# Moving split-off low parts to other engines, one softmax normalisation per step, and a new order of steps in a fused state-space and local-attention kernel

## The reference, cut to what matters

```python
xn = _layernorm(x)                      # x: 16 sequences x 256 tokens x 128
s = state_space_branch(xn)              # projections, convolutions, selective scan
for i in range(6):                      # DEPTH; 16 heads of 64, window of 32 tokens
    x = attn_layer(shift_tokens(x), Wqkv[i], q_scale[i], k_scale[i], Wo[i]) + x
    x = ffn_layer(shift_tokens(x), ln_g[i], ln_b[i], W1[i], b1[i], W2[i], b2[i]) + x
out = x0 + s * silu(x)

def attn_layer(x, Wqkv, qs, ksc, Wo):
    q, k, v = split(x @ Wqkv)           # 3 x 16 heads x 64
    q, k = l2norm(q) * qs, l2norm(k) * ksc
    q = q * cos * scale + rotate_half(q) * sin * scale
    k = k * cos / scale + rotate_half(k) * sin / scale
    return local_attention(q, k, v) @ Wo            # softmax(8 q k) v over a band

def ffn_layer(x, g, bln, W1, b1, W2, b2):
    xn = (x - mean) / sqrt(var + 1e-05) * g + bln
    a, gate = split(xn @ W1 + b1)
    return a * gelu(gate, approximate=False) @ W2 + b2
```

## Time and profile before

| | |
|---|---|
| median of 3 runs | 4315.71 us (4312.8 to 4320.33) |
| the profiled execution's own time | 4310.28 us |
| its span, first to last instruction | 4308.2 us |
| busy: TensorE, VectorE, ScalarE, GpSimd | 85%, 84%, 71%, 63% of the span |
| first and last `nb` instruction (line 1246) | 495.2 and 4219.4 us |

### The profile page before, as it was taken

One profiled execution on the slowest core, in us unless ns is written; L12 is line 12 of the kernel. 1 busy time (PEld: TensorE's weight loads), 2 busy tenths in 40 slices (PEclk: granted clock), 3 DMA queues, 4 the chain that ended last, 5 costly groups with the idle time before them and its releaser, 6 DMA issues. The chain is left out here.

```text
span 4308.2 us, 109724 instructions
## 1 busy us (share of the span) xinstructions
PE 3648.7 (85%) x31072; PEld 2319.1 (54%) x31072; DVE 3618.5 (84%) x12131; ACT 3063.5 (71%) x8807; POOL 2732.3 (63%) x4419
## 2 busy tenths in 40 slices
PE   5887688898888888888988888888888888898884
PEld 2444355555555555555555555555555555555552
DVE  7999688889888888888888888888887888888873
ACT  3443477777777777777787777777776777877774
POOL 0000577777777777677776776777776767777771
PEclk8999799999999999999999999999999999999997
DMA  1000322222222222222222222222222222222221
GB/s 45 6 7 12 106 92 90 85 90 96 90 88 90 82 95 93 87 93 84 84 101 91 93 87 80 88 95 88 99 84 79 94 95 89 94 85 89 86 78 61
DMA packets 225228, 352.55 MB, mean 82 GB/s; under 512 B 41535, under 2 KB 68349, under 8 KB 224381
## 3 DMA queue, kind: packets, MB, share of 16 engines
q1 hardware_dynamic: 224604, 345.22, 23.4%
HBM read 125.41 MB, written 5.77 MB: 30 GB/s over the span
## 5 line engine op out<-in xcount | busy, mean ns | idle before, releaser
L964 POOL TENSOR_SCALAR pr<-pr,rden 128x128 f32<-128x128 f32 (+1 forms) x3072 | 1134.4, 388 | 931.7 <-DVE rden L1219 930.6
L852 ACT ACTIVATE pr<-sm,nb,rq 128x128 f32<-128x128 f32 (+1 forms) x3072 | 1515.9, 498 | 44.7 <-DVE nb L1246 39.4
L971 POOL TENSOR_TENSOR rot<-ab,swp 128x512 f32<-128x512 f32 x768 | 984.4, 1282 | 509.7 <-DMA swp<-ab 508.5
L1194 DVE TENSOR_TENSOR ab<-bank,ltab 128x512 f32<-128x512 f32 x1536 | 985.4, 683 | 281.3 <-PE bank L292 260.8
L1240 DVE CUSTOM_DVE_ANT_0 sm<-bank,mask 128x128 f32<-128x128 f32 (+1 forms) x3072 | 841.3, 330 | 55.9 <-issue 52.2
L840 ACT ACTIVATE sq<-bank 128x512 f32<-128x512 f32 x768 | 451.6, 588 | 256.7 <-DVE ab L1194 255.0
L852 ACT ACTIVATION_READ_ACCUMULATOR pr<-sm,nb,rq 128x1 f32 x3072 | 587.8, 191 | 0.0
L634 PE MATMUL bank<-ident,pr 128*128 128x128 f32 x1536 | 407.1, 291 | 210.1 <-DVE pt L1226 208.3
L1226 DVE COPY pt<-bank 128x512 f32<-128x512 f32 x768 | 531.5, 692 | 10.2
L625 PEld LDWEIGHTS bank<-rot 64*64 64x64 f32 x12288 | 291.9, 133 | 452.8 <-issue 452.4
L977 POOL TENSOR_TENSOR rot<-rot,rkb 128x512 f32<-128x512 f32 x384 | 497.7, 1296 | 44.2 <-DMA rkb<-k_scratch 44.2
(11 more groups left out here) (156 smaller groups left out, 6503.7 us busy)
## 6 DMA issues: line engine op xcount, KB each, us to landing
swp<-ab SPq DMA_DIRECT2D x1536, 128.0 KB, 2.0
rkb<-k_scratch SPq DMA_DIRECT2D x768, 128.0 KB, 2.9
raw<-Wqkv SPq DMA_DIRECT2D x48, 128.0 KB, 2.2
gg<-xT SPq DMA_DIRECT2D x48, 128.0 KB, 2.3
gg<-xT SPq DMA_DIRECT2D x48, 127.5 KB, 2.4
raw<-Wqkv SPq DMA_DIRECT2D x12, 256.0 KB, 2.7
wo<-Wo SPq DMA_DIRECT2D x6, 512.0 KB, 4.2
k_scratch<-rsum SPq DMA_DIRECT2D x192, 8.0 KB
```

The source lines that it names most:

```text
L852: ins = act.activation(pr[:, s % 4, i, cs], sm[:, s % 2, i, cs], ACT.Exp, bias=nb[:, s, t, i:i + 1], scale=head_scale(rq, p, b)[:, t, i:i ...
L964: ins = pool.tensor_scalar(pr[:, e % 4, i, cs], pr[:, e % 4, i, cs], rden[:, e, t, i:i + 1], 1.0, ALU.mult, ALU.mult)
L971: pool.tensor_tensor(rot[:, PAIRS * (j % 2) + j // 2, :], ab[:, j % 2, 0, :], swp[:, j % 2, :], ALU.add).then_inc(qk_rot, 1)
L1194: ins = dve.tensor_tensor(seqs(ab[:, j % 2, i, :]), seqs(use_bank("qk", j)[:, :]), ltab[:, 2 * (j % 2) + i:2 * (j % 2) + i + 1, :] .to_bro ...
```

## The change

- x's parts for the group after next are no longer made on VectorE. `shift_next` (SyncE, step 8) writes the shifted x to a new buffer `xs2` with two DMAs, ScalarE makes the high part in one copy of 128x512 (step 11), GpSimd the low part in one subtraction (step 13).
- `split_low` of the weights moves from VectorE to GpSimd.
- `gate` is gone: Gelu reads the gate's bank itself, with the bias, so the gates' banks are free only after Gelu.
- `normalise` is one `tensor_tensor` per step, over 2x2x160 columns with `rden` broadcast, in place of four `tensor_scalar` of 128 or 160 columns. `pr` has 160 columns for each tile, the unused 32 being zero.
- Bank 7 is also used by q/k block 4 and gate 2; the sums of quads 0 and 2 become a use of that bank.
- Order: `cen` goes from TensorE's step 7 to 8, sum group 2 from 13 to 14, group 3 from 1 to 0, the third `dn` from 2 to 3, `norms(0)` from 9 to 8 on ScalarE; on VectorE `clamp` and `gated` come ahead of `maxima`, and `scale_q` one step earlier; GpSimd's `scale_k` of pair 7 goes from step 12 to 13, those of pairs 5 and 6 go one step earlier; k's norms go to DRAM one step earlier. `xs` has its own buffer, so that its zero column is written once.

```diff
-              [("prev", "cen", 0, 6), ("next", "qk", 7, 5)],
-              [("next", "qk", 8, 4), ("prev", "var", 0, 6)],
+ [('next', 'qk', 3, 5)], [('cur', 'rqT', 1, 4), ('next', 'qk', 4, 7)], [('next', 'qk', 5, 5), ('next', 'sum', 0, 7)],
+ [('next', 'qk', 6, 4)], [('next', 'qk', 7, 5)], [('next', 'qk', 8, 4), ('prev', 'cen', 0, 6), ('prev', 'var', 0, 6)],
...
+ [('prev', 'g', 0, 4), ('next', 'qk', 12, 5)], [('prev', 'g', 1, 6), ('prev', 'g', 2, 7), ('next', 'qk', 13, 5)],
+ [('prev', 'a', 0, 6), ('next', 'sum', 1, 7), ('prev', 'a', 1, 4), ('next', 'qk', 14, 5)],
+AT = {'wo': 2, 'shift': 5, 'residual': 6, 'centred': 7, 'ln_k': 8, 'norm': 10, 'high': 10, 'low': 11,
+ 'gelu': 13, 'gated': (15, 15, 16), 'down': (16, 17, 19), 'residual2': 19, 'clamp': (9, 2),
+ 'scale_q': (11, 4), 'k_out': (9, 2), 'q_norm': 2, 'next_shift': 8, 'next_high': 11, 'next_low': 13}
-QUAD_STEPS = {1: ("cur", 3), 5: ("next", 0), 8: ("next", 1), 13: ("next", 2)}
+QUAD_STEPS = {8: ('next', 1), 0: ('cur', 3)}
+SCALE_STEPS = {13: [('cur', 7), ('next', 0)], 15: [('next', 1)], 1: [('cur', 2)], 3: [('cur', 3)],
+ 6: [('cur', 4)], 7: [('cur', 5)], 9: [('cur', 6)]}
...
+                def shift_next(x):
+                    done = held(sp_e, n.n[1] + 2) if cur is not None else None
+                    src = seqs(xT[:, bass.ds(x * GT, GT)])
+                    if done is not None:
+                        sp_e.wait_ge(x_split, done)
+                    sp_e.dma_start(seqs(xs2[:, :])[0:64], src[0:64]).then_inc(xs2_in, 16)
+                    sp_e.dma_start(seqs(xs2[:, :])[64:128, :, 1:SEQ], src[64:128, :, 0:SEQ - 1]).then_inc(xs2_in, 16)
...
+                def split_high_x(buf):
+                    landed = held(act, n.z[32] + 64 if cur is not None else n.z[32] + 32)
+                    settle(act)
+                    act.wait_ge(xs2_in, landed)
+                    act.activation(xh[:, buf, :, :], seqs(xs2[:, :]), ACT.Copy).then_inc(x_hi, 1)
...
                 def gelu(q):
                     for c in range(3):
                         cn = FCH[c][1]
-                        act.wait_ge(f_gcp, n3 + (3 * q + c + 1))
-                        act.activation(gg[0:cn, c, :], gg[0:cn, c, :], ACT.Gelu).then_inc(f_gelu, 1)
+                        act.wait_ge(f_g, n3 + (3 * q + c + 1))
+                        act.activation(gg[0:cn, c, :], use_bank("g", c)[0:cn, :], ACT.Gelu,
+                                       bias=lv[0:cn, V_B1G + c:V_B1G + c + 1]).then_inc(f_gelu, 1)
...
-                    for i in range(2):
-                        for t in range(2):
-                            cs = slice(0, P) if t == 0 else slice(P, UW)
-                            ins = pool.tensor_scalar(pr[:, e % 4, i, cs], pr[:, e % 4, i, cs],
-                                                     rden[:, e, t, i:i + 1], 1.0, ALU.mult, ALU.mult)
+                    ins = pool.tensor_tensor(pr[:, e % 4, :, :, :], pr[:, e % 4, :, :, :],
+                                             rden[:, e, :, :].rearrange("p t i -> p i t").unsqueeze(3)
+                                             .to_broadcast([P, 2, 2, P + WINDOW]), ALU.mult)
...
+                def split_low_x(buf):
+                    made = held(pool, n1 + 3 if cur is not None else n1 + 2)
+                    settle(pool)
+                    pool.wait_ge(x_hi, made)
+                    pool.tensor_tensor(xl[:, buf, :, :], seqs(xs2[:, :]), xh[:, buf, :, :].bitcast(F32), ALU.subtract)\
+                        .then_inc(x_split, 1)
...
+                    if s - 1 in SPLIT_AT.get(kind, ()):
+                        split_low(nl, SPLIT_AT[kind][s - 1])
+                    if kind == "T2" and s in (1, 2):
+                        split_low(nl, 5 + s)
...
-                    if gs[2] is not None and s == 11:
-                        if cur is not None:
-                            dve.wait_ge(v_proj, n8 + 8)
-                        split_high_x(gs[2], par)
-                    if gs[2] is not None and s in (13, 14):
-                        split_low_x(gs[2], par, n1 + 3 if cur is not None else n1 + 2, s - 13)
```

More of the change, by code:

```diff
@@ new lines @@
+NWO = 4
+AT = {'wo': 2,
+ 'shift': 5,
+ 'residual': 6,
+ 'centred': 7,
+ 'ln_k': 8,
+ 'norm': 10,
+ 'high': 10,
+ 'low': 11,
+ 'gelu': 13,
+ 'gated': (15, 15, 16),
+ 'down': (16, 17, 19),
+ 'residual2': 19,
+ 'clamp': (9, 2),
+ 'scale_q': (11, 4),
+ 'k_out': (9, 2),
+ 'q_norm': 2,
+ 'next_shift': 8,
+ 'next_high': 11,
+ 'next_low': 13}
+V_STEPS = {1: ('cur', 4),
+ 3: ('cur', 5),
+ 5: ('cur', 6),
+ 7: ('cur', 7),
+ 9: ('next', 0),
+ 11: ('next', 1),
+ 13: ('next', 2),
+ 15: ('next', 3)}
+QUAD_STEPS = {8: ('next', 1), 0: ('cur', 3)}
@@ L937, in _ @@
                 split_high(0, c)
[L938 removed]
+            flow(act, turn, (1, 2, 3, 4, 8, 16), (32,))
             with act.Fori(0, GROUPS) as g:
@@ L955, in turn @@
                 z128, z256 = n.z[128], n.z[256]
+                nl = pool.snap(l + 1) if kind in ("load", "T0", "T2") else None
                 def normalise(e, q):
@@ L1009, in turn @@
                             scale_k(p, group_of(role, o))
+                    if s == AT["next_low"] and gs[2] is not None:
+                        split_low_x(par)
                     if prev is not None:
-                        if s == 10:
+                        if s == AT["norm"]:
                             normed(prev)
-                        if s == 11:
+                        if s == AT["low"]:
                             low(prev)
+            for c in range(CHUNKS):
+                split_low(0, c)
             pool.wait_ge(lv_ok, 1)
@@ L1315, in _ @@
+                    if kind == "T2" and s == AT["residual2"] - 15:
+                        layer_vectors(nl)
             for i in range(2):
```

182 lines of the change are left out of this document (88 added, 94 removed), and 4 rows, old and new, of the table BANK_STEPS.

## The result

The changed kernel takes 3999.14 us (median, 3994.67 to 4002.52), the kernel before 4314.26 beside it: a ratio of 0.9268, 95% interval [0.9252, 0.9284]. The forecast was 4111 with a range from 4010.

The account below looks back on a forecast made before the run. No single engine was taken as the bound; each stretch had its own. 45 turns x 4.9 = 220, plus 25 (weights) and 2 (end), less 45 given back, recorded as 204 off 4310.3: 4106, as median 4111; range 4010 to 4270.

Parts of the forecast that it names:

- the giving back of 45 us: Allowance of 1 us a turn for GpSimd's late step 13, weights' parts on top, and loop ends.
- 4.9 us a turn: Summed gain of all stretches in the turn shown: 70.9 us for a turn that took 75.8.
- 2→6: Steps 2 to 6, TensorE the bound: sum group and q/k block moves take 20.7 us to 19.9.
- 11→13: Steps 11 to 13: without VectorE's casts ahead of `copy_probs`, and `scale_q` earlier, 7.4 us, 2.4 less.
- 13→0: Step 13 to next step 0, ScalarE holds it: 16.8 us become 16.7; VectorE's 3 us give nothing.
- 0→2: Steps 0 to 2: `gated(2)` leaves VectorE and `clamp(1)` enters, 7.8 us as before.
- 8→11: Steps 8 to 11: centring matmul moves into step 8, `clamp(0)` ahead of `maxima(9)`; 12.3 us become 12.0.
- 6→8: Steps 6 to 8: centring no longer waits for the DMA; 8.28 us become 7.1.
- A: Rival: `normalise` at 2.0 us makes GpSimd level with the turn and late at step 13; 4268 us, chance 0.18.
- B: Rival: broadcast `normalise` makes GpSimd pace all steps, from 2.53 us per instruction; at 2.8, 4510 us, chance 0.05.
- C: Rival: `a` 0 and 1 wait for Gelus to free the gates' banks, lengthening 13→0; 4200 us, chance 0.12.
- D: Rival: TensorE is already the bound, waits come back at other places, nothing changes; 4316 us, chance 0.03.

Follow-up runs that it names:

- e1: The changed kernel with the weights' low parts back on VectorE: 4024.97 us.
- e2: The changed kernel plus an extra, unused GpSimd multiplication over 128 columns ahead of each `normalise`: 4044.84 us.
- e4: The changed kernel with x's high and low parts back on VectorE in steps 11, 13 and 14, without the two DMAs: 4164.49 us.
- e7: The changed kernel with the gates' copies back on ScalarE in steps 12 and 13, and Gelu reading what they wrote: 4113.53 us.
- g4: The changed kernel with only `gated` moved back behind `maxima` on VectorE: 4039.02 us.
- g1: The changed kernel with the fourth sum group back in step 1 and the third `dn` back in step 2: 4040.98 us.
- e5: The changed kernel with the centring matmul back in TensorE's step 7: 4033.56 us.
- i6: The changed kernel with block 13's `square` ahead of the second table load, `a` 0 and 1 swapping banks, layer norm's `Ln` and `Exp` a step later: 4008.48 us.
- g3: The changed kernel with only `clamp` moved back behind `maxima` on VectorE: 4093.91 us.
- i3: The changed kernel with the next block's shift taken at step 3, not step 8: 4001.56 us.
- f1: Old order and gate copies, with only the offloads and the single `normalise` of the change: 4264.0 us.
- f2: New order and Gelu from the bank only; x's and the weights' parts on VectorE, four normalisations a step: 4213.97 us.

## Why the forecast was right in direction and short in size

**The account.** Within the layers the forecast was 220 + 25 − 45 = 200, the trace gives 306.6. (With the two us for the end that is 202; the 204 on record is a slip of the sum.) Of the 306.6, the turn shown gives 45 x 5.5 = 247.5, the weights 26 (e1), and 33 are left. The missing 107 are the three terms below: 45, 27 and 33, and 1 on the weights.

- *The step that failed is the giving back of 45 us*, the largest of the three. It stood for GpSimd being late in step 13, at a `normalise` of 1.60 us. It measured 1.254, and `scores(14)` do not wait. The mechanism was right: e2, which brings the 1.60 about, shows just this wait and costs 46 us. What failed was the size, by the choice of the row: two full inputs (2.50 ns a column) for a broadcast one (1.96). That 46 and 45 agree is luck, since the 45 were a round 1 us a turn, which stood for loop ends and the weights' parts too. The turn shown gave its 5.5 us with nothing given back.
- *4.9 us a turn was 5.5.* 27 us in 45 turns. In the turn shown 2→6 gave 1.45 (forecast 0.8), 11→13 2.68 (2.4), 13→0 0.33 (0.1) and 0→2 0.14 (0), while 8→11 lost 0.30 where 0.3 was to be won; 6→8 gave 1.23 (1.2).
- *45 turns of one kind.* 33 us: the first three turns gained 2.2, 4.2 and 5.1, which the forecast left out (11.5), the rest, some 21, are in turns longer than the one that it worked with. Mean turns gained 6.7 us (78.65 to 71.93), the one shown 5.5. The prediction had the sign of it in its own rows: a pace of 77.6 us a turn beside a turn of 75.8.

**The stretches**, in the prediction's order, means of 44 turns; what was forecast to go stands in brackets:

- 11→13: −2.70 (−2.4). Right, mechanism and size: steps 11 and 12 at 3.58 and 3.65; in the turn shown the clock is 1.00.
- 13→0: −0.45 (−0.1). Right in that ScalarE holds it and that VectorE's 3 us give nothing (e4: 13→15 unchanged). But the small net hides large parts: without the gate copies leaving it would be 1.7 us longer (e7), and VectorE now comes there earlier and waits more, 8.50 us in step 14.
- 0→2: −1.03 (0). "`gated` 0 and 1 and `gated` 2 only change sides of `maxima`" was costed at nothing. g4 puts `gated` at 40 us; 0 to 1 takes 1.1 us less with it ahead, given back in part at 14 to 15.
- 2→6: −0.98 (−0.8). Right: the sums and the third `dn` are worth 42 us (g1).
- 6→8: −1.81 (−1.2), 8→11: +0.25 (−0.3). The DMA wait is gone and worth 34 us (e5). What is new in 8→11 is 0.85 us in step 10: 0.2 are `scale_q`, the rest is VectorE's wait for ScalarE, late from `norms` in step 8; it goes when the layer norm's part comes a step later (3.75 us in i6). The prediction carried this lateness to step 13 and charged it there, and not in step 10. It also counted `clamp(0)` ahead of `maxima(9)` as a small cost on VectorE; with `norms` in step 8 the two places are 95 us apart (g3). Whether the earlier `norms` is itself worth anything, no run shows.

**GpSimd.** Forecast 62.7 us a turn; by the records above it is 16 x (1.254 + 1.281) + 10.3 + 3.3 + 1.3 + 1.3 = 56.8, and 5.6 of the difference are the 16 x 0.35 us of `normalise`. (The windows give it 2610.8 us in 48 turns, 54.4 each, since each record overlaps the next by some 0.03 to 0.05 us.) It is busy for 76% of the layers, where 85% were forecast. In the turn shown it idles 0.8 us in 8→11 and then not at all until late in step 14, as feared, and yet TensorE hardly waited for it in the layers (0.2 us by name). VectorE did. One of the prediction's signs of being wrong was VectorE waiting for `rotate`, and it does so once a turn (us in total, times, longest):

```profile
DVE ab L1262 <- POOL rot L1028: 31.0, 47, 3.3
```

In the turn shown that is 0.60 us in step 8. So GpSimd's lateness is not quite without a price even at 1.254 us; what it costs in the end was not measured.

**SyncE** at nothing: right. ScalarE's copy that reads the two DMAs' result (L937, 47 times) had no idle time before it, and their place makes no difference (i3).

**The rivals.** A needed 2.0 us; at 1.6 the cost is 46 us, at 2.2 it is 202. B's point was not reached, see above. C is there as a wait (59.6 us) but not as a loss against the gate copies (e7). D falls: 76 us of waiting for the DMA and 150 for `copy_probs` went, and the time with them.

**What stays open.** The parts undone singly add up to more than the gain (26 + 165 + 22 + 114 + 185 = 512, for 315), done by halves to less (53 + 106). That fits a stretch as long as its slowest engine, where each part shows its worth only with the others' limit gone; the tables of f1 and f2 show it at 11→13 and 13→0, not at every place. Why the turns differ among each other less after the change was not looked into, nor how much of each price is the granted clock, beyond the places named above, nor where `normalise` would bring the time back to that of before.

## What to carry to other kernels

Where an instruction is moved, ask who waits for it and not only how long it is: moving a clamp of 0.7 us past the maxima changes nothing in VectorE's own sum and cost 95 us in the run, since another engine's queue stood behind it. Price an edit by several turns and not by the tidiest one: here the turn worked with gave 5.5 us and the mean turn 6.7. Count TensorE's busy time beside its waits, since a stretch with a long wait may also run at a lower clock (busy time is 103 of the 306 us here). And an unknown price that is allowed for as a lump (here 45 us) is best measured alone: two runs with an added instruction gave two points of what it costs, 46 us at 1.6 and 202 at 2.2.
